# Graph attention in one kernel: products 4 to 7 split around the spread, and bfloat16 parts written by ScalarE

## The reference

```python
h = (x @ W).reshape(N, 8, 32)
alpha_s = einsum('nhc,hc->nh', h, a_src); alpha_d = einsum('nhc,hc->nh', h, a_dst)
e = alpha_s[src] + alpha_d[dst]
e = where(e > 0, e, 0.2 * e)
m = segment_max(e, dst)
ex = exp(e - m[dst])
alpha = ex / (segment_sum(ex, dst) + 1e-16)
out = segment_sum(h[src] * alpha[:, :, None], dst).reshape(N, 256) + b
```

## Time and profile before

| | us |
|---|---|
| median of 3 runs | 3269.58 (3264.3 to 3275.27) |
| the profiled execution | 3246.74 |
| its span | 3244.9 |
| first attention round | about 1463 to 2175 of the span |
| second attention round | about 2302 to 3017 of the span |

### The profile page before, as it was taken

The page is one execution under the profiler, slowest core; times in us unless marked ns, Lnnn a source line. Parts: engine busy times, 40 slices in busy tenths (PEclk is TensorE's granted clock), DMA queues, the critical chain, the costliest instruction groups (busy, mean ns, idle before and its releaser), DMA issues.

```text
span 3244.9 us, 37834 instructions
## 1 busy us (share of the span) xinstructions
PE 1871.6 (58%) x10306; PEld 1535.4 (47%) x10306; DVE 1558.5 (48%) x5038; ACT 926.1 (29%) x2028; POOL 1398.2 (43%) x1415
## 2 busy tenths in 40 slices
PE   7998244444568999614444443454344444444599
PEld 6887133323458999513333333343233333333377
DVE  4200133323486555715555555574455555555854
ACT  4444575665013444311111111113111111111432
POOL 1000756666503443254554555504555455452143
PEclk9999666666768999867776767776676777677699
DMA  6444555555238999643333333313333343332000
GB/s 215 192 195 194 183 172 172 193 186 167 82 80 309 353 352 346 215 131 109 116 116 109 117 115 113 117 45 119 105 113 116 111 119 115 110 114 86 1 14 27
DMA packets 207423, 473.88 MB, mean 146 GB/s; under 512 B 33230, under 2 KB 100370, under 8 KB 200750
## 3 DMA queue, kind: packets, MB, share of 16 engines
q0 software_dynamic: 63520, 179.35, 19.6%
q1 hardware_dynamic: 112878, 190.07, 16.5%
q10 hardware_dynamic: 30816, 101.99, 8.8%
HBM read 367.19 MB, written 104.90 MB: 145 GB/s over the span
## 4 chain that ended last, share of the span: by engine, by line
PE 31%; another core or an unknown queue 29%; DVE 25%; issue 11%; DVEq 3%; DMA 1%; POOL 1%; ACT 0%; ACTq 0%; SPq 0%; POOLq 0%
PE banks L421 8%; PE banks L1209 7%; DVE arena L1606 3%; PE banks L1221 3%; DVE arena L1694 3%; PE banks L802 3%; DVE arena L1659 2%; DVE arena L816 2%; DVEq L696 2%; DVEq L699 1%; DVE X L825 1%; PE banks L1375 1%; DVE xn L1618 1%; PE banks L2113 1%
## 5 line engine op out<-in xcount | busy, mean ns | idle before, releaser
L1416 POOL DMA_INDIRECT arena<-ht,srcT x784 | 779.4, 994 | 743.5 <-DVE arena L1694 447.5
L774 POOL DMA_INDIRECT arena<-tr,idx1T x392 | 373.8, 954 | 399.9 <-DMA tr<-arena 207.9
L802 PE MATMUL banks<-arena 128*128 x884 | 266.8, 465 | 330.2 <-DVE arena L816 206.7
L1523 PE MATMUL banks<-arena,XT 128*128 128x264 f32 x884 | 354.6, 490 | 178.1 <-DVE arena L1694 71.6
L802 PEld LDWEIGHTS banks<-arena 128*128 128x128 f32 x884 | 201.1, 235 | 396.0 <-issue 362.8
L1511 PE MATMUL banks<-arena 128*128 128x25 bf16 x896 | 32.6, 182 | 595.2 <-issue 595.2
L1524 PE MATMUL banks<-arena,XT 128*128 128x264 f32 x884 | 329.8, 461 | 0.0
L1694 DVE TENSOR_TENSOR arena<-arena,nrmT 128x528 f32<-128x528 f32 x448 | 312.7, 701 | 20.3 <-ACT nrmT L1472 19.3
L1523 PEld LDWEIGHTS banks<-arena,XT 128*128 128x128 f32 x884 | 203.5, 243 | 237.1 <-issue 120.5
L1511 PEld LDWEIGHTS banks<-arena 128*128 128x128 bf16 x896 | 28.5, 104 | 601.5 <-issue 601.5
L825 DVE TENSOR_TENSOR X<-X,banks 128x256 f32 x221 | 91.5, 414 | 407.6 <-remote 380.7
(11 more groups left out here) (364 smaller groups left out, 3279.7 us busy)
## 6 DMA issues: line engine op xcount, KB each, us to landing
arena<-in_L_ffn_w_dram SPq DMA_DIRECT2D x195, 512.0 KB
tr<-arena SPq DMA_DIRECT2D x50, 1024.0 KB, 3.9
XT<-otd ACTq DMA_DIRECT2D x52, 512.0 KB
arena<-ohd ACTq DMA_DIRECT2D x52, 512.0 KB
arena<-dld ACTq DMA_DIRECT2D x28, 512.0 KB
otd<-arena ACTq DMA_DIRECT2D x28, 512.0 KB
ohd<-arena ACTq DMA_DIRECT2D x28, 512.0 KB
arena<-ht,srcT POOLq DMA_INDIRECT x784
```

What stands on the lines that cost most here:

```text
L774: pool.indirect_dma_start(Gr[:, o:o + D], None, TR, bass.IndirectOffsetOnAxis(ap=idx1T[:, q:q + 1], axis=0)).then_inc(d_g[b % NG], 16)
L802: mm = ten.matmul(B[n][:, 0:D], OHr[:, n, h, :], Gr[:, h * D:][:, bass.ds(o, D)], start=(h == 0), stop=(h == 1))
L1416: pool.indirect_dma_start(Gall[:, o:o + ROW], None, HT[L], bass.IndirectOffsetOnAxis(ap=srcT[:, q:q + 1], axis=0)).then_inc(d_g[b % NG], 16)
L1523: ten.matmul(B[n][:, 0:MSG], OH[b][:, 2 * j, :], WG[:, j, 0, :], start=True, stop=False)
```

## The change

`pause(n)` is a list of n empty turns for `weave`. On DVE the three casts of tables(n) and the three of ends(q) go: ACT writes these parts, and DVE keeps the subtractions between them, so that each cut becomes ACT, DVE, ACT, DVE, ACT over two new semaphores (`left_ok`: DVE has left a value; `part_ok`: ACT has written a part). The column of flags of SB moves from 8 to 24, so that values(q) sums three parts in one tensor_reduce in place of a copy and two adds. DVE's order becomes tables(n) woven with across(q), three empty turns and then adds(c, 0..3). weigh leaves out the steps past the 221st.

PE's order becomes: products(c, 4..5), expand(n), scores(q), back(q), products(c, 6..7) with the second `pr_ok`, maxima(q), products(n, 0..3). ACT's order becomes: offsets(q), the table parts of n, the exponential of fc, scores(q), the parts of ends(q), the exponential of the weights, three DMA issues, widen(q).

The hunks outside the attention only let `sort_end` and `id_ok` share semaphores with others and are left out here.

```diff
@@ -68,6 +68,11 @@
...
 
+def pause(n):
+    for _ in range(n):
+        yield
+
+
 def none():
...
@@ -1351,6 +1357,7 @@
...
         d_ob = sems("d_ob", 2)
+        left_ok, part_ok = sem("left_ok"), sem("part_ok")
 
...
@@ -1438,12 +1445,40 @@
...
         def act_gat(L):
-            def scores(c):
-                k = L * NCH + c
+            def offsets(c):
                 ga_.load(c * CH)
...
                 act.reg_alu(more2, more, ET * (L + 1), ALU.add)
+
+            def parts_of_tables(c):
+                k = L * NCH + c
+                left, part = 5 * k + 2, 4 * k + 2
+                act.load([into], doff[48][0:1, c * CH:c * CH + 1])
+                o = act.snap(into, min_val=0, max_val=(NS - 1) * 48)
+                to = TB[:, bass.ds(o, 48 * CH)].rearrange("p (n c) -> p n c", c=48)
+                if c:
+                    act.wait_ge(spread_ok, k)
+                act.wait_ge(left_ok, left + 1)
+                act.copy(to[:, :, 8:16], heads_of(ln_)).then_inc(part_ok, 1)
+                act.wait_ge(left_ok, left + 2)
+                act.copy(to[:, :, 24:32], heads_of(tmid)).then_inc(part_ok, 1)
+                act.wait_ge(left_ok, left + 3)
+                act.copy(to[:, :, 40:48], heads_of(tmid)).then_inc(sp_ok, 1)
+
+            def parts_of_ends(c):
+                k = L * NCH + c
+                if c:
+                    act.wait_ge(mx_ok, k)
+                act.wait_ge(sm_ok, k + 1)
+                act.copy(SB[:, :, 0:8], SM).then_inc(part_ok, 1)
+                act.wait_ge(left_ok, 5 * k + 1)
+                act.copy(SB[:, :, 8:16], SM).then_inc(part_ok, 1)
+                act.wait_ge(left_ok, 5 * k + 2)
+                act.copy(SB[:, :, 16:24], SM).then_inc(sb_ok, 1)
+
+            def scores(c):
+                k = L * NCH + c
                 act.wait_ge(ld_ok, more2)
...
@@ -1462,16 +1497,22 @@
...
                 if 0 <= q < NCH:
-                    scores(q)
+                    offsets(q)
                 if 0 <= n < NCH:
+                    parts_of_tables(n)
                     if n:
...
                         act.activation(fc, fc, ACT.Exp).then_inc(f_ok, 1)
-                    widen(n)
+                if 0 <= q < NCH:
+                    scores(q)
+                    parts_of_ends(q)
+                if 0 <= n < NCH:
                     act.wait_ge(x_in, L * NCH + n + 1)
...
                         ends_and_places(act, L, n + 2)
+                if 0 <= q < NCH:
+                    widen(q)
 
...
@@ -1495,13 +1536,15 @@
...
 
-            def maxima(c):
-                b, k = c % 2, L * NCH + c
-                ten.wait_ge(scan_ok, k + 1)
+            def back(c):
+                ten.wait_ge(scan_ok, L * NCH + c + 1)
                 for n in range(2):
...
                 t.then_inc(back_ok, 1)
+
+            def maxima(c):
+                b, k = c % 2, L * NCH + c
                 ten.wait_ge(d_ob[b], 16 * (L * NCH // 2 + c // 2 + 1))
...
@@ -1528,14 +1571,19 @@
...
                 c_on, n_on, q_on = (0 <= k < NCH for k in (c, n, q))
-                if q_on:
-                    scores(q)
                 if n_on:
...
                 if c_on:
-                    products(c, 4, 8).then_inc(pr_ok, 1)
+                    mm = products(c, 4, 6)
+                    if steps_of(c) < 7:
+                        mm.then_inc(pr_ok, 1)
                 if n_on:
                     expand(n).then_inc(spread_ok, 1)
+                if q_on:
+                    scores(q)
+                    back(q)
+                if c_on and steps_of(c) > 6:
+                    products(c, 6, 8).then_inc(pr_ok, 1)
                 if q_on:
...
@@ -1578,22 +1626,27 @@
...
                 yield
-                v = leaky(ln_, ln_, v)
+                vec.wait_ge(dv.sem, v)
+                vec.scalar_tensor_tensor(ln_, ln_, 0.2, ln_, ALU.mult, ALU.max).then_inc(left_ok, 1)
                 yield
...
                     yield
+                k = L * NCH + c
+                o = TB[:, bass.ds(tb_.at(c * CH), 48 * CH)].rearrange("p (n c) -> p n c", c=48)
+                vec.wait_ge(part_ok, 4 * k + 3)
+                vec.tensor_tensor(heads_of(tmid), heads_of(ln_), o[:, :, 8:16], ALU.subtract).then_inc(left_ok, 1)
+                yield
+                if c:
                     vec.wait_ge(dv.sem, f)
                     vec.tensor_tensor(fc, lo_, ln_[:, 0:8], ALU.subtract).then_inc(f_in, 1)
-                    vec.wait_ge(spread_ok, L * NCH + c)
-
-                def place(t):
-                    o = TB[:, bass.ds(tb_.at(c * CH), 48 * CH)].rearrange("p (n c) -> p n c", c=48)
-                    return o[:, :, 8 + 16 * t:16 + 16 * t]
-
-                yield from thirds(place, heads_of(ln_), heads_of(tmid), sp_ok, v)
+                    yield
+                o = TB[:, bass.ds(tb_.at(c * CH), 48 * CH)].rearrange("p (n c) -> p n c", c=48)
+                vec.wait_ge(part_ok, 4 * k + 4)
+                vec.tensor_tensor(heads_of(tmid), heads_of(tmid), o[:, :, 24:32], ALU.subtract).then_inc(left_ok, 1)
+                yield
 
...
@@ -1624,13 +1677,19 @@
...
                 yield
-                vec.wait_ge(sm_ok, k + 1)
-                yield from thirds(lambda t: SB[:, :, (0, 9, 17)[t]:(8, 17, 25)[t]], SM, SM, sb_ok, 0)
+                yield
+                vec.wait_ge(part_ok, 4 * k + 1)
+                vec.tensor_tensor(SM, SM, SB[:, :, 0:8], ALU.subtract).then_inc(left_ok, 1)
+                yield
+                yield
+                vec.wait_ge(part_ok, 4 * k + 2)
+                vec.tensor_tensor(SM, SM, SB[:, :, 8:16], ALU.subtract).then_inc(left_ok, 1)
+                yield
 
...
                 la = laT[:, c * CC:(c + 1) * CC].rearrange("p (s o) -> p s o", o=1)
-                dv.put(vec.tensor_copy(SB[:, :, 8:9], la))
+                dv.put(vec.tensor_copy(SB[:, :, 24:25], la))
                 yield
...
@@ -1638,14 +1697,10 @@
...
                 vec.wait_ge(mx_ok, k + 1)
-                v = dv.put(vec.tensor_scalar(vp, pm[:, :, 8], -1.0, BIG, ALU.add, ALU.mult))
+                v = dv.put(vec.tensor_scalar(vp, pm[:, :, 24], -1.0, BIG, ALU.add, ALU.mult))
                 yield
-                u = dv.put(vec.tensor_copy(VV, pm[:, :, 17:25]))
+                u = dv.put(vec.tensor_reduce(VV, pm[:, :, 0:24].rearrange("p s (t h) -> p s h t", h=8), AX, ALU.add))
                 yield
-                for t in (9, 0):
-                    vec.wait_ge(dv.sem, u)
-                    u = dv.put(vec.tensor_tensor(VV, VV, pm[:, :, t:t + 8], ALU.add))
-                    yield
                 vec.wait_ge(dv.sem, u)
...
@@ -1688,11 +1743,11 @@
...
                 vec.wait_ge(x_ok, k + 1)
-                for j in range(CH):
+                for j in range(steps_of(c)):
                     gm = block_at(gv_.at(c * CH + j))[:, :, 0:MSG].rearrange("p a (h c) -> p a h c", c=HW)
...
                     vec.tensor_tensor(WG[:, j].rearrange("p a (h c) -> p a h c", c=HW), gm, ex.to_broadcast([P, 2, 8, HW]),
-                                      ALU.mult).then_inc(w_ok, 1)
+                                      ALU.mult).then_inc(w_ok, 1 + CH - steps_of(c) if j + 1 == steps_of(c) else 1)
                     if j == 1:
...
@@ -1717,7 +1772,7 @@
...
                 c_on, n_on, q_on = (0 <= k < NCH for k in (c, n, q))
-                weave(tables(n) if n_on else none(), chain(adds(c, 0, 4) if c_on else none(), across(q) if q_on else none()))
+                weave(tables(n) if n_on else none(), chain(across(q) if q_on else none(), pause(3), adds(c, 0, 4) if c_on else none()))
                 scan = ends(q) if q_on else none()
...
```

More of the change, by code:

```diff
@@ L460, in build @@
         recv = {k: (H if k == "nrm" else H.bitcast(I32))[0:RW, 0:4 * RL].rearrange("p (j k) -> p j k", k=4) for k in names}
-        s_in, s_rec, s_back, s_se, s_io, s_hi, s_mm, s_pos, s_raw, s_wd, s_end = (sem("sort_" + n) for n in (
-            "in", "rec", "back", "se", "io", "hist", "mm", "pos", "raw", "used", "end"))
+        s_in, s_rec, s_back, s_se, s_io, s_hi, s_mm, s_pos, s_raw, s_wd = (sem("sort_" + n) for n in (
+            "in", "rec", "back", "se", "io", "hist", "mm", "pos", "raw", "used"))
         def unsorted(eng, body):
@@ L489, in pool_sort @@
             pool.wait_ge(s_se, 64)
-            pool.memset(flagf[:, 1:2], 0.0).then_inc(s_end, 1)
-            pool.wait_ge(s_end, 1)
+            pool.memset(flagf[:, 1:2], 0.0).then_inc(s_io, 1)
+            pool.wait_ge(s_io, 2)
         def pe_sort():
@@ L906, in build @@
         d_gp = sem("d_gp")
-        ix_ok, id_ok, fr_ok, ec_ok, er_ok = (sem(n) for n in ("ix_ok", "id_ok", "fr_ok", "ec_ok", "er_ok"))
+        ix_ok, fr_ok, ec_ok, er_ok = (sem(n) for n in ("ix_ok", "fr_ok", "ec_ok", "er_ok"))
         d_cb, d_c2 = sems("d_cb", 2), sem("d_c2")
@@ L1030, in dve_routing @@
                                   ALU.mult).then_inc(ix_ok, 1)
-            vec.wait_ge(id_ok, 1)
+            vec.wait_ge(er_ok, 2)
```

(3 more changed lines are left out.)

## The result

The changed kernel takes 3379.99 us (median of 6 runs, 3368.93 to 3388.2). The kernel before beside it takes 3269.41 (6 runs): ratio 1.0337, 95% interval 1.0316 to 1.0357, slower by some 110 us. I had forecast 3338, within 3228 to 3392. The profiled execution took 3380.58, with a span of 3378.8.

The account below looks back on a forecast made before the run. It took waits as the bound: PE signals held until a burst of gathers ends, then the chain to weigh. Terms of +65, +3, +5 and -4 us made +69 on 3269.6: 3339, rounded 3338, range 3228 to 3392.

Parts of the forecast that it names:

- The path: Attention rounds: work inside a burst of gathers is free; work between PE's signal's release and the next weigh is paid fully.
- Casts, tables and ends: 0: Moving DVE's casts of tables and ends to ACT gains or costs 0 by itself.
- Scan and turn-back behind the release: DVE's scan, now held with the spread, runs after the release; PE's turn-back is there at release + 1.25 us.
- Products 6 and 7: On PE behind the turn-back at 1.2 GHz, 3.5 us; first weigh 5.3 us after release against 3.42, +1.9 a gap.
- Short bursts: + 0.3: After a burst of 8 gathers PE may still run at 2.4 GHz, so ten such gaps cost 0.3 us each.
- Values: -0.2 a gap: One reduction replaces three DVE operations in values; about -0.2 us of it is on the path.
- Without gathers and last chunk: +5 - 4: Six chunks with no gather in flight cost 0.8 us each, +5; weigh's shorter last chunk saves 2.1 us a round, -4.
- The sum: Over both attention rounds: long bursts +65, short +3, without gathers +5, last chunk -4, together +69 us.
- hold: A PE signal that comes late in a burst of gathers reaches nobody until the burst ends, about 2.4 us behind it.
- The early slip (1): The scan's signal passes inside the burst, so scan, turn-back, products 6 and 7 run there: -38 us, 3232; chance 0.18.
- Dearer round trips (4): ACT's parts and the scan come on top of the products: +2.7 us a gap, +130, 3400; chance 0.14.
- Rival 2: PE's earlier spread gets through in the burst, weighs begin before its end in a third of chunks: -149 us, 3120; chance 0.08.

Follow-up runs that it names:

- e1: The changed kernel with PE's order of before and ACT's scores first, casts still on ACT: 3243.19 us against 3245.16 for the kernel before, 0.9994.
- e3: The changed kernel with scores(q) first again on PE and ACT, products 6 and 7 still behind the turn-back: 3187.1 us, 0.9825 of the kernel before.
- e2: The kernel before with PE's new order and nothing else: 3268.32 us, 1.0087 of the kernel before.
- e4: The kernel before with POOL pausing (six small memsets, each waited for) ahead of every second block of gathers: 3050.37 us, 0.9395.
- e5: The changed kernel with the casts of the tables back on DVE: 2694.16 us, 1.0059 of the kernel before at 2681.29.
- e10: The changed kernel with the casts of the tables back on DVE, run again on a third chip: 2694.36 us, 1.005 of the kernel before.
- e11: The changed kernel with the casts of the tables back on DVE, a third time: 2691.12 us against 2680.6 for the kernel before, 1.0043.
- e9: The changed kernel itself, run again on a third chip: 2689.95 us against 2680.4 for the kernel before, 1.0036.
- e8: The kernel before with shorter POOL pauses (two memsets for six) ahead of every second block of gathers: 2758.31 us, 1.0287 of the kernel before.
- e12: The changed kernel with scores(q) first again on PE and ACT, plus two-memset POOL pauses ahead of every second block: 2750.59 us, 1.0253 of the kernel before.

## Why the prediction was right, and where not

- *The path.* Right, and e1 to e3 bear it out in the account: the gathers' wait for weigh is 447.5 us before, 441.9, 472.7 and 395.6 in e1, e2 and e3, and 564.3 after. Against before that is -6, +25, -52 and +117 us; the times moved by -2, +23, -58 and +111. All of it is set against the one profile of the kernel before, whose execution (3246.74) is close to the runs beside e1 to e4 and some 23 us under those beside the changed kernel.
- *Casts, tables and ends: 0.* Right by themselves (e1, where DVE's order and values are changed too).
- *Scan and turn-back behind the release.* Seen as forecast: turn-back from + 0.74 to + 1.21, and DVE goes on behind it at + 1.25.
- *Products 6 and 7.* Mechanism right, size short. Two cold steps put the add at + 5.06 (forecast 4.8), and between add and weigh lie 0.35 us of issue where I had booked 0.08. The first weigh comes at + 5.84, not 5.3: + 2.4 instead of + 1.9 us a gap.
- *Short bursts: + 0.3.* This step failed: PE is as cold after 4.16 us of idling, and the first weigh is at + 5.83.
- *Values: -0.2 a gap.* Nothing of it shows in the gap: it grew by 2.43, the first weigh came 2.42 later.
- *Without gathers and last chunk: +5 - 4.* Short: from the last release of a hold to the end of the last weigh a round takes 65.4 and 64.9 us against 62.4 and 62.3, +5.6 for both in place of +1.
- *The sum.* With these, 48 x 2.43 = 117 in place of 65 + 3. The profiled executions lie 134 us apart, the medians 111. Of the other 17 of the former, 5.6 are the ends of the rounds, and 10.0 lie ahead of the first gather of the attention (1395.75 before, 1405.77 after), in layers that the change leaves alone.
- *What held it together.* I took for granted that a signal late in a burst is held to its end. In the changed kernel that is so in 22 of the 24 bursts of the first round (25 waits, 319 us); with the order alone it is so in 12 (e2: 23 waits, 207.9 us). That the premise held just here, when it already failed in 3 of 24 bursts of the trace it was read from, was luck. The order alone brings + 0.9%, the rest alone nothing, and both + 3.4%, the last on other runs and perhaps another chip than the first two. Which part of the rest (the casts on ACT, ACT's later scores, DVE's order) makes the scan's hold last isn't settled.
- *What stays open.* e5 was made to tell whether it is the tables' way through ACT that makes the hold last, and its three runs (e5, e10, e11) fell on chips without the hold. Its theory was that a signal sent later in the burst is held to the end. As one fixed point in the burst the traces rule that out: of the scans whose scores' row ended 9.5 to 11.9 us after the start of a long burst, 12 of 14 came through inside it in e2 and none of 9 in the changed kernel.
- *Rivals.* The early slip (1) came true in half of e2's bursts and, for the spread, in 14 of e3's 24, but in only 2 of the change's. Dearer round trips (4) aren't seen: DVE's waits for ACT's parts are under 6 us a round. By the number alone, 3380 us, it lies nearer (3400) than my forecast (3338), whose own range of 3310 to 3370 the result misses by 10 us; what speaks for the forecast is the path, and not the number. Rival 2, much faster, didn't come. Of its two grounds, PE starting its matmuls late in a burst is not seen: the spread and the scores start 0.41 us apart in a burst of the changed kernel (1942.07, 1942.48) and 0.43 in e9 (1703.85, 1704.28). Since a row's end is modelled, the rows can't tell whether the last matmul ends late or only its signal is. The Trainium skill (Perfetto Trace Analysis, Tensor Engine Instruction) puts a matmul's signal behind the acknowledged write to PSUM. The 0.11 us between row and waiter in e9 fit that, and where on this way the signal is held no run shows.

## What to carry to other kernels

A wait for "remote" that begins with a matmul's end and ends 2.5 us behind a series of indirect DMAs is worth an experiment of its own before any order is tuned around it: breaking the series with pauses of POOL gave 6% on the chip of e4, while the reordering moved from -1.8 to +3.4%. On chips without the hold shorter pauses cost 2.9% (e8). Keep signals that others need for their next step ahead of the ones that are going to be held, and put on the far side only what nobody asks for. And measure on more than one chip: the same change costs 3.4% on one and 0.4% on another.

## What the runs showed of the hardware

- The kernel before takes 3245 to 3270 us on the chips of the first runs and of e1 to e4, and 2680 to 2681 on two others (e5 to e8, e9 to e12). Of the changed kernel, gathers take 995 ns on the one kind and 1013 on the other (e9), and a pair of products' matmuls 1.09 or 0.61 us on both; what differs is when PE's signals arrive in long series of gathers. Of the some 570 us between the two kinds for the kernel before, 447.5 are POOL's wait for weigh, and 73 more stand before the gathers of the first layer (idle 399.8 us after the change on the one, 327.0 on the other; for 52.0 of it the releaser is "remote" and isn't known to be PE). The kernel before has no profile on the other kind of chip, and the remaining 50 or so are not taken apart. What sets the chips apart isn't known.
- Signals between ACT and DVE pass during the gathers on the chip with the hold: DVE's wait for ACT's table parts (L1640 <- L1463) is 0.4 us at most in the first round of the changed kernel.
- On a chip with the hold a signal of PE is delivered 0.8 us late between series of 4 gathers with stops of 1.8 us (e4's chunk). In a series of 16 it was 5 us late and still within the series in e2's chunk, 12.0 us late and 2.4 us behind the series in that of the earlier trace rows.
- A good part of the price of the chain after a release is PE's clock: for 9 us from the release it is granted 0.68 on the mean,

```profile
1977.00:1986.00 9.00, 6.76 (x34) 4.84 (x34) 6.75 (x22) 3.10 (x5) 0.16 (x1) 0.68 0.35 118
```

  the first two steps at 1.2 GHz (1.09 us a pair), the next at 2.4 (0.61). The same two steps take 2.0 us in e9 at the higher level (1705.78 to 1707.82), and 3.9 here (1978.21 to 1982.10).
